# Second mixture's dispatch of half 0 moved into the last three chunks of the state space stage

## The chip, the cores and the metric

The program runs on one core of a Trainium2 chip. The metric is the device time of one execution in microseconds (us), taken as the median of several executions. Five engines run beside each other, each with a queue of its own that is worked off in order: TensorE (PE), VectorE (DVE), ScalarE (ACT), GpSimd (POOL) and SyncE (SP, which here only issues transfers). They wait for each other by semaphores.

## The reference, cut to what matters

4096 rows of 128 numbers pass four layers, each added to its input: an attention, a first mixture of experts, a selective state space layer, and a second mixture of experts. The last two are what the change is about:

```python
x = x + _L1_attn_ref(_layernorm(x, axis=-1), ...)      # state space, 16 states per channel, scan over time
x = x + _L1_ffn_ref(_layernorm(x, axis=-1), ...)       # second mixture
# _L1_ffn_ref, x of shape (4096, 128), 8 experts of width 176, the best 2 taken
scores = jax.nn.softmax(xf @ gate_w.T, axis=-1)
biased = scores + gate_b
_, idx = lax.top_k(biased, K)
w = jnp.take_along_axis(scores, idx, axis=-1) * ROUTER_SCALE
h = jax.nn.silu((xf @ w1 + b1) * (xf @ w3 + b3))       # per chosen expert
y = sum over the 2 chosen experts of w * (h @ w2 + b2)
z = _expert(xf, sw1, sb1, sw3, sb3, sw2, sb2)          # one shared expert for all rows
return y + z
```

The state space layer works on 16 sequences of 256 rows, and no sequence needs another.

## The kernel before

All rows stay in SBUF as `X`: 32 tiles of 128 rows. Half 0 is tiles 0 to 15, half 1 is tiles 16 to 31.

**State space stage** (`state_space`). The 16 sequences are worked on in 8 chunks `c` of two sequences (512 rows, four tiles), so that chunks 0 to 3 are half 0. A chunk has 16 steps `n`, one for each state, in which the two halves `h` of the channels are gone through. In each step ACT makes `dA` by two exponentials (line 1781, three steps ahead), DVE makes `dBu` by two products (1907) and runs two scans into `Hs` (1915, four buffers), POOL multiplies them by `Cb` into `HC` (1871, two buffers), and PE adds `HC` up in PSUM (1621, in `accumulate`, one step later). DVE waits at step `n` for the products `HC` of step `n-4`, POOL waits for PE's sum of step `n-2`. SP loads `Bb` and `Cb` for two steps at a time (`load`), the next `Bb` behind the `Cb` that waits for POOL. Beside that, the queues hold the next chunk's preparation: POOL's four `softplus_step` at steps 3 to 6, PE's projections at steps 0 to 2 and 8 to 10, and at step 2 of a chunk DVE's `gate_rows` of the chunk before (line 1890, `yg`), whose output projection and `update` of `X` (1895) follow at steps 4 and 6. Each `for n in range(N)` loop is written out by Python, so that what stands in it under `if (c, n) == ...` stands at that one place of the engine's queue. After the last step PE, DVE, PE and DVE finish the last chunk one after the other.

**Dispatch of the second mixture** (`dispatch`, a block of its own behind the state space stage). Class `Dispatch` has the steps, each named by its engine. For a half of the rows: DVE takes the mean and variance (`vector_stats`, `vector_variance`), ACT the root, DVE the factor (`vector_scales`) and the normalised rows (`vector_rows`) into `XS`; PE transposes these (`tensor_turn`), ACT copies them (`scalar_copy`), PE multiplies by the router (`tensor_score`); DVE chooses two experts for each row (`vector_keep`, `vector_choose`), PE counts (`tensor_rank`), and DVE works out to which row of the table `rows1` in HBM each row goes (`vector_slots`, `vector_tables`). Then POOL sends the rows: `pool_reweight` puts the first weight beside them, and `pool_scatter` issues one indirect DMA for each of the 16 tiles; then the same for the second choice, when the first 16 have landed. The table was filled with zeros at the kernel's start. The block holds this for half 0 on DVE, ACT, PE and POOL, and for half 1 all but POOL's part.

**Experts** (`experts`). At the start of its block POOL waits until half 0's rows have landed and releases SP (`placed`), which loads 39 tiles of the table; PE, ACT and DVE work them off, while POOL sends half 1's rows by 32 scatters. Half 1's 39 tiles, the shared expert and 64 indirect gathers back into `X` end the program.

A `with nc.Block()` ends for all engines when the last of them is through.

Of the kernel before, what the change touches and what calls it, by code (L numbers as in the profile page):

```python
# [595 lines left out]
class Dispatch:  # L596
# [36 lines left out]
    def over(self, halves, stats, batches, by_scalar, kept_by_scalar):  # L633
# [75 lines left out]

    def tensor_turn(self, pe, k, rows, count):  # L710
# [123 lines left out]
    def pool_reweight(self, pool, h, k):  # L834
# [5 lines left out]
        self.nc.gpsimd.tensor_copy(self.XS[:, half, D], self.rt.c[k][:, half]).then_inc(s.reweighted.sem, 1)  # L840
# [3 lines left out]
    def pool_scatter(self, pool, k, lo, hi, op):  # L844
        for t in range(lo, hi):
            self.nc.gpsimd.indirect_dma_start(self.XG, bass.IndirectOffsetOnAxis(self.rt.slot[k][:, t:t + 1], 0),  # L846
                                              self.XS[:, t, :], None, compute_op=op).then_inc(self.s.sent.sem, 16)


def dispatch(nc, tag, d):  # L850
# [6 lines left out]
    with ExitStack() as ctx:  # L857
        m = Maker(nc, ctx, tag)
        TP = [m.ps(f"TP{v}", [P, d.G * P]) for v in range(2)]
        RP, RK, TT = m.ps("RP", [P, HT * E]), m.ps("RK", [P, HT * E]), m.ps("TT", [P, HT * E])  # L860
        d.place(TP, RP[:], RK[:], TT[:])
        with nc.Block() as block:
            @block.vector
            def _(dve):
                d.vector_stats(dve, 0, HT)
                d.vector_variance(dve, 0, 0, HT)
                d.vector_scales(dve, 0, 0, HT)
                d.vector_rows(dve, 0, HT)
# [14 lines left out]
            def _(act):  # L883
                for h in range(2):
                    d.scalar_root(act, h, h * HT, (h + 1) * HT)
                    for g in range(d.HG):
                        d.scalar_copy(act, h * d.HG + g)
                    d.scalar_power(act, h)

            @block.tensor  # L890
            def _(pe):
                for h in range(2):
                    for g in range(d.HG):
                        k = h * d.HG + g
                        d.tensor_turn(pe, k, d.s.rows, (k + 1) * d.G)
                    if h == 1:
                        pe.wait_ge(d.s.kept.sem, d.s.kept.after(0))
                    for g in range(d.HG):
                        d.tensor_score(pe, h * d.HG + g, g * d.G)
                    if h == 1:  # L900
                        pe.wait_ge(d.s.counted.sem, d.s.counted.after(0))
                    d.tensor_rank(pe, h)
# [1236 lines left out]
```

## Time and profile before

| | us |
|---|---|
| median of 3 runs | 1254.69 |
| lowest, highest | 1253.68, 1259.11 |
| the profiled execution | 1261.0 |
| its span in the trace | 1259.1 |

Busy shares of the span: PE 79%, DVE 75%, POOL 66%, ACT 58%. The span can be cut by stages: the state space stage up to 974 us, the dispatch block from 974 to 1051 us, the experts of the second mixture from 1051 us on. A row of the timeline gives the start, the duration, the engine, the line, what is written from what, and in brackets how long the engine had been idle and what ended that. `x4` is four instructions merged, whose duration is that of all. `SPq` is the queue of transfers that SP issues.

### The profile page before, as it was taken

The numbers are of one execution on the slowest core, as the hardware profiler recorded it, in microseconds if no ns is written. First come the engines' busy times: TensorE is split into PE (matmuls) and PEld (weight loads), VectorE is DVE, ScalarE is ACT, GpSimd is POOL, SyncE is SP. The second block draws the span as 40 slices with busy tenths as digits, with TensorE's granted clock in tenths as the row PEclk, the third lists the DMA queues.
The fourth block names the chain that finished last, engine by engine and source line by source line (L and its number), as shares of the span: only waits on it lengthen the run. The fifth ranks groups of instructions, "written<-read, shape, count | busy, mean of one in ns | idle before, by whom it ended". The sixth has DMA issues, their size and how long they took to land. (4 is left out here: it accounts for less than half of the span.)

```text
span 1259.1 us, 17033 instructions
## 1 busy us (share of the span) xinstructions
PE 998.2 (79%) x4202; PEld 606.3 (48%) x4202; DVE 942.2 (75%) x2310; ACT 735.4 (58%) x1636; POOL 830.8 (66%) x604
## 2 busy tenths in 40 slices
PE   5888867489999978888888888898776335999970
PEld 4666755368888723333333333333222333777750
DVE  6999999653333437999898989999998743777760
ACT  4777747265555568776667676867531113777740
POOL 3333248557247275989898978787975077767676
PEclk9999989599999979999898989989989556999995
DMA  9993012246435343353544443444542014756543
GB/s 271 177 168 124 1 10 24 40 60 92 73 77 94 69 80 104 111 170 116 164 125 153 137 124 126 160 130 140 168 150 67 2 49 76 120 104 123 106 93 64
DMA packets 139137, 133.50 MB, mean 106 GB/s; under 512 B 14579, under 2 KB 120163, under 8 KB 138915
## 3 DMA queue, kind: packets, MB, share of 16 engines
q1 hardware_dynamic: 107106, 115.55, 34.2%
q0 software_dynamic: 31936, 16.86, 11.4%
q8 instruction: 39, 0.64, 0.2%
q14 instruction: 56, 0.45, 0.1%
HBM read 98.66 MB, written 31.60 MB: 103 GB/s over the span
## 5 line engine op out<-in xcount | busy, mean ns | idle before, releaser
L1871 POOL TENSOR_TENSOR ss_HC<-ss_Hs,ss_Cb 128x512 f32<-128x512 f32 x256 | 324.8, 1365 | 85.0 <-PE ss_Y L1621 64.4
L1621 PE MATMUL ss_Y<-ss_HC,g_ident 128*128 128x512 f32 x512 | 270.4, 649 | 47.3 <-POOL ss_HC L1871 41.0
L1915 DVE TENSOR_TENSOR_SCAN ss_Hs<-ss_dA,ss_dBu 128x512 f32<-128x512 f32 x256 | 296.8, 1200 | 7.7 <-ACT ss_dA L1781 7.7
L846 POOL DMA_INDIRECT rows<-m_XS,g_slot x128 | 174.3, 1362 | 61.7 <-issue 34.6
L1781 ACT ACTIVATE ss_dA<-ss_delta,g_A 128x510 f32<-128x510 f32 x256 | 168.3, 712 | 74.1 <-DVE ss_Hs L1915 73.9
L1621 PEld LDWEIGHTS ss_Y<-ss_HC,g_ident 128*128 128x128 f32 x512 | 92.9, 200 | 209.2 <-POOL ss_HC L1871 149.2
L1153 PE MATMUL m_x_UP<-g_m_w,m_x_gT 128*128 (+1 forms) x532 | 193.0, 469 | 0.0
L1907 DVE TENSOR_TENSOR ss_dBu<-ss_duP,ss_Bb 128x512 f32<-128x512 f32 x256 | 163.1, 682 | 10.5 <-DMA ss_Bb<-bc_rows 8.9
L1173 PEld LDWEIGHTS m_x_DP<-g_m_w,m_x_hT 128*128 128x128 f32 x908 | 121.9, 191 | 62.3 <-issue 34.6
L1173 PE MATMUL m_x_DP<-g_m_w,m_x_hT 128*128 (+1 forms) x908 | 140.7, 284 | 2.4 <-ACT m_x_hT L1245 2.3
L1245 ACT ACTIVATE m_x_hT<-m_x_HP 128x256 f32<-128x256 f32 (+1 forms) x188 | 80.3, 427 | 87.7 <-PE m_x_HP L1163 85.9
L1294 DVE SCALAR_TENSOR_TENSOR m_x_hid<-m_x_UP,m_x_G,m_x_sg 128x352 f32<-128x352 f32 x78 | 45.5, 583 | 110.2 <-ACT m_x_sg L1227 110.2
L1133 POOL DMA_INDIRECT g_X<-out_rows,g_slot x64 | 100.4, 1569 | 38.1 <-issue 18.3
L520 POOL TENSOR_TENSOR at_RP<-at_RP,a_rope 128x1024 f32<-128x1024 f32 x16 | 38.4, 2401 | 90.3 <-ACT at_RP L357 90.2
L1153 PEld LDWEIGHTS m_x_UP<-g_m_w,m_x_gT 128*128 128x128 f32 x532 | 87.9, 194 | 18.3 <-issue 1.7
L1163 PE MATMUL m_x_HP<-g_ident,m_x_hid 128*128 128x128 f32 x454 | 80.6, 273 | 2.5 <-DVE m_x_hid L1294 2.5
L1301 DVE TENSOR_TENSOR m_x_sg<-m_x_UP,g_m_b 128x352 f32<-128x352 f32 x110 | 57.7, 524 | 33.2 <-PE m_x_UP L1153 33.1
L1121 POOL DMA_INDIRECT g_X<-out_rows,g_slot x32 | 49.3, 1541 | 44.8 <-DMA out_rows<-m_x_YO 33.6
L1144 PE MATMUL m_x_TP<-g_ident,m_x_G 128*128 128x128 f32 x188 | 52.5, 279 | 30.0 <-DMA m_x_G<-rows 28.8
L1586 PE MATMUL ss_Q<-ss_xpad,ss_w_conv 128*128 128x512 f32 x128 | 60.5, 619 | 5.2 <-ACT ss_xpad L1711 5.2
L1227 ACT ACTIVATE m_x_sg<-m_x_UP 128x352 f32<-128x352 f32 x78 | 36.2, 464 | 39.7 <-PE m_x_UP L1153 39.7
L1163 PEld LDWEIGHTS m_x_HP<-g_ident,m_x_hid 128*128 128x128 f32 x454 | 56.0, 142 | 4.0 <-DVE m_x_hid L1294 2.8
(271 smaller groups left out, 1760.9 us busy)
## 6 DMA issues: line engine op xcount, KB each, us to landing
ss_Bb<-bc_rows SPq DMA_DIRECT2D x64, 512.0 KB, 5.0
ss_Cb<-bc_rows SPq DMA_DIRECT2D x64, 512.0 KB, 4.1
rows<-g_Z SPq DMA_DIRECT2D x2, 5031.0 KB, 48.9
m_x_G<-rows SPq DMA_DIRECT2D x156, 64.5 KB
out_rows<-m_x_YO SPq DMA_DIRECT2D x156, 64.0 KB
g_m_w<-in_w_up SPq DMA_DIRECT2D x1, 2816.0 KB, 11.2
g_m_b<-in_b SPq DMA_DIRECT2D x1, 2160.0 KB, 10.3
g_X<-in_x SPq DMA_DIRECT2D x4, 512.0 KB, 5.8
```

Source lines behind the costliest of these rows:

```text
L846: self.nc.gpsimd.indirect_dma_start(self.XG, bass.IndirectOffsetOnAxis(self.rt.slot[k][:, t:t + 1], 0), self.XS[:, t, :], None, compute_op ...
L1133: nc.gpsimd.indirect_dma_start(X[:, t * D:(t + 1) * D], None, Y[0:(h + 1) * NH * P, :], bass.IndirectOffsetOnAxis(rt.slot[k][:, t:t + 1], ...
L1153: ins = nc.tensor.matmul(UP[v % 2][:, at:at + n], gT[v % 2][:], w.w[:, ds(e + c, n)], start=True, stop=True)
L1163: ins = nc.tensor.transpose(HP[0:n, c * P:(c + 1) * P], hid[v % 2][:, c0:c0 + n], ident[:])
L1173: ins = nc.tensor.matmul(DP[v % 2][:, 0:D], hT[v % 2][0:n, c * P:(c + 1) * P], w.w[0:n, ds(e + WU + c * D, D)], start=c == 0, stop=c == NC ...
L1245: ins = nc.scalar.activation(hT[v % 2][:, 0:full], HP[:, 0:full], ACT.Copy)
L1586: ins = nc.tensor.matmul(dst, w_conv[:, h, k, :], xpad[:, h, :, k:k + S], start=k == 0, stop=k == K)
L1621: ins = nc.tensor.matmul(Yp[:, h, :], ident[:], HC[n % 2][:, h, :], start=False, stop=n == N - 1)
L1781: nc.scalar.activation(dA[n % NA][:, h, :, 1:S], seqs(delta[v][:, h, :])[:, :, 1:S], ACT.Exp, scale=A[:, h, n:n + 1]).then_inc(dA_ready.se ...
L1871: nc.gpsimd.tensor_tensor(HC[n % 2][:, h, :], Hs[n % 4][:, h, :], Cb[g % 2][:, n % 2, :], ALU.mult).then_inc(hc_ready.sem, 1)
L1907: v_.tensor_tensor(dBu[:, h, :], duP[:, h, :], Bb[g % 2][:, n % 2, :], ALU.mult).then_inc(dBu_ready.sem, 1)
L1915: v_.tensor_tensor_scan(Hs[n % 4][:, h, :], dA[n % NA][:, h, :, :].rearrange("p s t -> p (s t)"), dBu[:, h, :], 0.0, ALU.mult, ALU.add).th ...
```

## The change

Half 0's dispatch leaves the block behind the state space stage and is written into the state space loops: at chunk 5 (`OWN - 1`), chunk 6 (`OWN`) and chunk 7 (`LAST`). Eight (`sent`) of its 32 scatters are issued there too, one for each of steps 5 to 12 of chunk 7. In the block that is left, POOL begins at once with the other 24 scatters, and the other engines do half 1's dispatch. The normalised rows of half 0 are now made by ACT (`scalar_rows`), not DVE, with one more DVE instruction (`vector_minus`); groups have four tiles in place of eight; the eight early scatters add to the zeros in the table, the others write. `XS` is split in two tensors. Waiting for the mixture's weights now stands ahead of the state space stage.

```diff
+    def vector_minus(self, dve, lo, hi):
+        self.nc.vector.scalar_tensor_tensor(self.minus[:, lo:hi], self.mv[:, lo:hi, 0], -1.0, self.sc[:, self.n - 1, lo:hi],
+                                            ALU.mult, ALU.mult).then_inc(self.s.scaled.sem, 1)
...
+    def vector_less(self, dve):
+        v, link = self.nc.vector, Chain(dve, self.chain)
+        link(v.tensor_reduce(self.mx[:], self.lg[:], AX.X, ALU.max))
+        v.tensor_tensor(self.ex[:], self.lg[:], self.each(self.mx), ALU.subtract).then_inc(self.s.less.sem, 1)
+
     def vector_choose(self, dve, h):
+        self.vector_less(dve)
+        self.vector_pick(dve, h)
+
+    def vector_pick(self, dve, h):
...
@@ dispatch
             @block.vector
             def _(dve):
-                d.vector_stats(dve, 0, HT)
-                d.vector_variance(dve, 0, 0, HT)
-                d.vector_scales(dve, 0, 0, HT)
-                d.vector_rows(dve, 0, HT)
                 d.vector_stats(dve, HT, T)
                 d.vector_variance(dve, 1, HT, T)
-                d.vector_keep(dve, 0, 0)
-                d.vector_choose(dve, 0)
-                d.vector_slots(dve, 0)
-                d.vector_tables(dve, 0)
                 d.vector_scales(dve, 1, HT, T)
                 d.vector_rows(dve, HT, T)
+                d.vector_tables(dve, 0)
                 d.vector_keep(dve, 1, 1)
                 d.vector_choose(dve, 1)
                 d.vector_slots(dve, 1)
...
             @block.gpsimd
             def _(pool):
-                for k in range(2):
-                    d.pool_reweight(pool, 0, k)
-                    d.pool_scatter(pool, k, 0, HT, ALU.bypass)
+                d.pool_scatter(pool, 0, sent, HT, ALU.bypass)
+                d.pool_reweight(pool, 0, 1)
+                d.pool_scatter(pool, 1, 0, HT, ALU.bypass)
...
@@ state_space, tensor
+                        if (c, n) == (LAST, 0):
+                            d.tensor_rank(pe, 0)
+                        if (c, n) == (LAST, 4):
+                            pe.wait_ge(d.s.counted.sem, d.s.counted.after(0))
...
+                        if (c, n) == (OWN, 7):
+                            pe.wait_ge(x_updated.sem, x_updated.after(c - 1))
+                        if c == OWN and 7 <= n < 7 + d.HG:
+                            d.tensor_score(pe, n - 7, (n - 7) * d.G)
+                        if (c, n) == (OWN, 6):
+                            pe.wait_ge(gate_copied.sem, gate_copied.after(c + 1))
+                        if c == OWN and 6 <= n < 6 + d.HG:
+                            d.tensor_turn(pe, n - 6, d.s.scalar_rows, (n - 5) * d.G)
...
@@ state_space, scalar
+                        if (c, n) == (OWN - 1, 13):
+                            d.scalar_root(act, 0, 0, HT)
+                        if c == OWN and 3 <= n < 3 + d.HG:
+                            d.scalar_rows(act, 0, (n - 3) * d.G, (n - 2) * d.G)
+                        if c == OWN and 7 <= n < 7 + d.HG:
+                            d.scalar_copy(act, n - 7)
+                        if (c, n) == (OWN, 14):
+                            d.scalar_power(act, 0)
...
@@ state_space, gpsimd
+                        if (c, n) == (LAST, 4):
+                            d.pool_reweight(pool, 0, 0)
+                        if c == LAST and 5 <= n < 5 + sent:
+                            d.pool_scatter(pool, 0, n - 5, n - 4, ALU.add)
...
@@ state_space, vector
+                        if (c, n) == (OWN - 1, 12):
+                            d.vector_stats(dve, 0, HT)
+                            d.vector_variance(dve, 0, 0, HT)
+                        if (c, n) == (OWN, 0):
+                            d.vector_scales(dve, 0, 0, HT)
+                            d.vector_minus(dve, 0, HT)
+                        if (c, n) == (OWN, 14):
+                            d.vector_keep(dve, 0, 0)
+                            d.vector_less(dve)
+                        if (c, n) == (LAST, 0):
+                            d.vector_pick(dve, 0)
+                        if (c, n) == (LAST, 3):
+                            d.vector_slots(dve, 0)
```

POOL's queue from chunk 7 of the state space stage to its end. The first fence is of before (L1871 the `HC` products, L846 the scatters of the second mixture, L1133 the last gathers):

```order
L1871 TENSOR_TENSOR ss_HC<-ss_Hs,ss_Cb 128x512 x50
L1527 UNCONDITIONAL_BRANCH
L904 UNCONDITIONAL_BRANCH
L840 COPY m_XS<-g_c 128x16
L846 DMA rows<-m_XS,g_slot 9984x129 x16
L840 COPY m_XS<-g_c 128x16
L846 DMA rows<-m_XS,g_slot 9984x129 x16
L862 UNCONDITIONAL_BRANCH
L1102 UNCONDITIONAL_BRANCH
```

The second is of the change; of the eight pairs of a scatter and its step's products the first two and the last stand here.

```order
L1892 TENSOR_TENSOR ss_HC<-ss_Hs,ss_Cb 128x512 x28
L852 COPY m_XS<-g_c 128x16
L1892 TENSOR_TENSOR ss_HC<-ss_Hs,ss_Cb 128x512 x2
L858 DMA rows<-m_XS,g_slot 9984x129
L1892 TENSOR_TENSOR ss_HC<-ss_Hs,ss_Cb 128x512 x2
L858 DMA rows<-m_XS,g_slot 9984x129
...
L858 DMA rows<-m_XS,g_slot 9984x129
L1892 TENSOR_TENSOR ss_HC<-ss_Hs,ss_Cb 128x512 x6
L1528 UNCONDITIONAL_BRANCH
L902 UNCONDITIONAL_BRANCH
L858 DMA rows<-m_XS,g_slot 9984x129 x8
```

In the second, products of the state space stage stand behind each of the eight scatters, and the block that follows starts with a scatter in place of a wait.

DVE's queue in chunk 7 of the change, from step 3 to step 4: L1932 is `dBu`, L1940 the scans, and between them stands `vector_slots`, of which the first seven and the last two instructions stand here.

```order
L1940 SCALAR_TENSOR_TENSOR ss_Hs<-ss_dA,ss_dBu 128x512 x2
L810 COPY m_d_tot<-ss_Q 128x128
L811 COPY m_d_rk<-ss_Q 128x128
L812 SCALAR_TENSOR_TENSOR m_d_run<-g_masks,m_d_tot 128x128
L814 TENSOR_TENSOR m_d_base<-m_d_run,m_d_tot 128x128
L815 TENSOR_SCALAR m_d_n_i<-m_d_run 128x8
L816 TENSOR_SCALAR m_d_n_i<-m_d_n_i 128x8
L817 CAST m_d_ct<-m_d_n_i 128x8
...
L829 CAST g_slot<-m_d_mx 128x16
L830 CAST g_slot<-m_d_mx 128x16
L1932 TENSOR_TENSOR ss_dBu<-ss_duP,ss_Bb 128x512 x2
L1940 SCALAR_TENSOR_TENSOR ss_Hs<-ss_dA,ss_dBu 128x512 x2
```

Before, the scans of step 3 and the `dBu` of step 4 stood next to each other there.

## Rows read from the trace of the kernel before

**Rows 1.** Stretches: busy us and instructions by engine, PE clock, DMA share, GB/s

```profile
860.00:918.00 58.00, 43.59 (x92) 15.51 (x91) 56.30 (x66) 36.56 (x51) 50.61 (x38) 0.92 0.46 147
1006.00:1051.00 45.00, 10.92 (x50) 10.21 (x50) 16.71 (x66) 3.64 (x4) 30.93 (x33) 0.50 0.14 47
```

**Rows 2.** Timeline of the dispatch block, POOL's rows and SP's first load behind it

```profile
1005.53 1.06 POOL L846 DMA_INDIRECT rows<-m_XS,g_slot  x1 [4.96 <-DVE g_slot L818]
...
1027.39 0.21 POOL L840 COPY m_XS<-g_c 128x16 f32<-128x16 f32 x1 [1.56 <-DMA rows<-m_XS,g_slot]
...
1028.12 0.98 POOL L846 DMA_INDIRECT rows<-m_XS,g_slot  x1 [0.52 <-POOL m_XS L840]
...
1047.20 0.96 POOL L846 DMA_INDIRECT rows<-m_XS,g_slot  x1 [0.30 <-issue]
...
1051.15 4.86 SPq L1076 DMA_DIRECT2D m_x_G<-rows  x6
```

**Rows 3.** Timeline of the dispatch block, DVE's part for half 0

```profile
974.26 3.19 DVE L664 BATCH_NORM_STATS2 m_d_st<-g_X 128x6 f32<-128x128 f32 x16 [0.71 <-PEq L79]
...
979.15 0.25 DVE L685 RECIPROCAL m_d_sc<-m_d_t 128x16 f32<-128x16 f32 x1 [0.28 <-ACT m_d_t L679]
...
980.27 4.19 DVE L700 TENSOR_SCALAR m_XS<-g_X,m_d_mv,m_d_sc 128x128 f32<-128x128 f32 x16
...
993.15 0.29 DVE L756 COPY m_d_lg<-m_f_RP 128x128 f32<-128x128 f32 x1 [4.17 <-PE m_f_RP L735]
...
994.46 0.29 DVE L741 TENSOR_REDUCE m_d_sm<-m_d_ex 128x16 f32<-128x128 f32 x1 [0.37 <-ACT m_d_ex L747]
...
1004.62 0.17 DVE L818 CAST g_slot<-m_d_mx 128x16 int32<-128x16 f32 x1
```

**Rows 4.** Timeline, POOL in two steps of chunk 7, and DVE behind the last step

```profile
945.22 2.49 POOL L1871 TENSOR_TENSOR ss_HC<-ss_Hs,ss_Cb 128x512 f32<-128x512 f32 x2 [0.89 <-DVE ss_Hs L1915]
...
952.06 2.49 POOL L1871 TENSOR_TENSOR ss_HC<-ss_Hs,ss_Cb 128x512 f32<-128x512 f32 x2 [0.89 <-DVE ss_Hs L1915]
...
969.50 1.23 DVE L1890 TENSOR_TENSOR ss_yg<-ss_Y,ss_gate 128x1024 f32<-128x1024 f32 x1 [2.80 <-PE ss_Y L1621]
```

**Rows 5.** Timeline, POOL in chunk 2: a gather between the products of its steps

```profile
655.00 4.95 POOL L1871 TENSOR_TENSOR ss_HC<-ss_Hs,ss_Cb 128x512 f32<-128x512 f32 x4 [0.72 <-PE ss_Y L1621]
660.11 1.57 POOL L1852 DMA_INDIRECT g_X<-out_rows,g_slot  x1 [0.15 <-issue]
661.11 5.50 POOL L1871 TENSOR_TENSOR ss_HC<-ss_Hs,ss_Cb 128x512 f32<-128x512 f32 x4
```

**Rows 6.** Timeline of chunk 0, POOL and DVE: small DVE instructions between the scans

```profile
506.50 2.51 POOL L1871 TENSOR_TENSOR ss_HC<-ss_Hs,ss_Cb 128x512 f32<-128x512 f32 x2
507.15 0.67 DVE L1408 TENSOR_SCALAR sr_ve<-sr_mv 128x8 f32<-128x8 f32 x1
507.74 1.31 DVE L1409 TENSOR_SCALAR sr_ve<-sr_mv 128x8 f32<-128x8 f32 x1
508.95 2.38 POOL L1521 TENSOR_TENSOR ss_delta<-ss_delta,ss_ln 128x1024 f32<-128x1024 f32 x1
508.96 2.40 DVE L1410 COPY g_mean<-sr_mv 128x8 f32<-128x8 f32 x1
```

**Rows 7.** Timeline of chunks 6 and 7: a late load, and PE's and POOL's waits

```profile
896.52 1.30 DVE L1907 TENSOR_TENSOR ss_dBu<-ss_duP,ss_Bb 128x512 f32<-128x512 f32 x2 [1.71 <-DMA ss_Bb<-bc_rows]
...
919.49 3.55 PE L1618 MATMUL ss_Y<-ss_xi,ss_w_D 128*128 128x512 f32 x4 [6.48 <-DVE ss_yg L1890]
...
924.90 12.33 POOL L1871 TENSOR_TENSOR ss_HC<-ss_Hs,ss_Cb 128x512 f32<-128x512 f32 x10 [6.25 <-PE ss_Y L1621]
```

**Rows 8.** Timeline, PE: half 0's transposes and scores in the block, a wait in chunk 6

```profile
982.47 4.02 PE L716 MATMUL m_f_TP<-g_ident,m_XS 128*128 128x128 f32 x16 [9.64 <-DVE m_XS L700]
...
986.28 6.83 PE L735 MATMUL m_f_RP<-g_m_wr,m_d_xT 128*128 128x8 f32 x32
...
885.18 3.64 PE L1621 MATMUL ss_Y<-ss_HC,g_ident 128*128 128x512 f32 x4 [2.40 <-POOL ss_HC L1871]
```

More of the change, by code:

```diff
@@ L649, in over, with row @@
             s.lifts.over(batches)
+    def row(self, t):
+        return self.XS[t // HT][:, t % HT, :]
     def each(self, a):
@@ L706, in scalar_rows @@
         for t in range(lo, hi):
-            self.nc.scalar.activation(self.XS[:, t, 0:D], self.X[:, t * D:(t + 1) * D], ACT.Identity, bias=self.minus[:, t:t + 1],
+            self.nc.scalar.activation(self.row(t)[:, 0:D], self.X[:, t * D:(t + 1) * D], ACT.Identity, bias=self.minus[:, t:t + 1],
                                       scale=self.sc[:, use, t:t + 1]).then_inc(self.s.scalar_rows.sem, 1)
@@ L846, in pool_scatter, with dispatch @@
             self.nc.gpsimd.indirect_dma_start(self.XG, bass.IndirectOffsetOnAxis(self.rt.slot[k][:, t:t + 1], 0),
-                                              self.XS[:, t, :], None, compute_op=op).then_inc(self.s.sent.sem, 16)
-def dispatch(nc, tag, d):
+                                              self.row(t), None, compute_op=op).then_inc(self.s.sent.sem, 16)
+def dispatch(nc, tag, d, sent):
     with ExitStack() as ctx:
         m = Maker(nc, ctx, tag)
-        TP = [m.ps(f"TP{v}", [P, d.G * P]) for v in range(2)]
+        TP = [m.ps(f"TP{v}", [P, d.G * P]) for v in range(d.HG)]
         RP, RK, TT = m.ps("RP", [P, HT * E]), m.ps("RK", [P, HT * E]), m.ps("TT", [P, HT * E])
@@ L883, in _ @@
             def _(act):
[L884 to L888, printed above, removed]
+                d.scalar_root(act, 1, HT, T)
+                for k in range(d.HG, 2 * d.HG):
+                    d.scalar_copy(act, k)
+                d.scalar_power(act, 1)
             @block.tensor
             def _(pe):
[L892 to L902, printed above, removed]
+                for g in range(d.HG):
+                    d.tensor_turn(pe, d.HG + g, d.s.rows, (g + 1) * d.G)
+                for g in range(d.HG):
+                    d.tensor_score(pe, d.HG + g, g * d.G)
+                d.tensor_rank(pe, 1)
             @block.gpsimd
             def _(pool):
-                for k in range(2):
-                    d.pool_reweight(pool, 0, k)
-                    d.pool_scatter(pool, k, 0, HT, ALU.bypass)
+                d.pool_scatter(pool, 0, sent, HT, ALU.bypass)
+                d.pool_reweight(pool, 0, 1)
+                d.pool_scatter(pool, 1, 0, HT, ALU.bypass)
 class TileSignals:
@@ L924, in over, with experts @@
         self.y_ready.over(routed)
-def experts(nc, tag, signals, d, inside, X, XS, rt, XG, Y, out, n_early, w, gated, ident, ahead=None):
+def experts(nc, tag, signals, d, inside, X, rt, XG, Y, out, n_early, w, gated, ident, ahead=None):
     n_shared, scale_col, H = w.n_shared, w.ns, w.H
@@ L1070, in fetch @@
                     if t.shared:
[L1071 removed]
+                        sp.dma_start(G[v][:, 0:D], d.row(t.i)[:, 0:D]).then_inc(arrived[v], 16)
                     else:
@@ L1464, in state_space @@
         Q = [m.ps(f"Q{v}", [P, CH]) for v in range(2)]
+        d.place([Q[1]], Q[0][:, 0:HT * E], Q[0][:, HT * E:2 * HT * E], Q[0][:, 2 * HT * E:3 * HT * E])
+        OWN, LAST = NCH - 2, NCH - 1
         padded, cleared, weights_ready = m.sem("padded"), m.sem("cleared"), m.sem("weights_ready")
```

35 lines of the change are left out of this document (16 added, 19 removed).

## The prediction

> **What bounds the kernel now.** I cut the span into stretches first. In chunk 6 DVE is busy for 56.30 of 58.00 us, so it sets the pace of the state space stage and anything given to DVE there is paid in full; POOL has 50.61 of the 58. In the later part of the dispatch block only POOL works much, DVE for 16.71 of 45 us [rows 1]. Then the timelines of that block. DVE begins half 0 at 974.26 [rows 3]; POOL issues its first scatter at 1005.53, comes to the second set of 16 at 1028.12 and ends its last at 1048.16; SP's first load for the experts follows at 1051.15 [rows 2]. So the block costs 76.9 us: 31.3 in which POOL waits for slots, 42.6 of POOL, 3.0 of block end. Nothing of the experts can start earlier, since POOL's queue stands in front of the block's end. The stage behind it is not touched by the change: the same 39 tiles, the same 32 scatters, the same gathers. It shifts as a whole.
>
> **The block: what is taken out.** A scatter's pitch is (1047.20 - 1028.12) / 15 = 1.27 us. Before, 16 scatters and their landing took 1027.39 - 1005.53 = 21.86 us [rows 2]. Now POOL starts with the block, with 8: 21.86 - 8 x 1.27 = 11.7. The weights' copy and the wait behind it take 0.73 (1027.39 to 1028.12), the other 16 take 20.04 (to 1048.16), the end of the block 2.99. Sum 35.5, from 76.9: **41.4 us less**. Beside it DVE does for half 1 what it did for half 0, from 974.26 to 1004.79 [rows 3], 30.5 us and a little over 1 for the tables at its end; half 0's tables lie in its wait for the scores (4.17 us idle at 993.15). That is 32, and POOL's own part is 11.7 + 0.7 + 20.0 = 32.5. POOL stays last, but by less than 1 us: more scatters moved out would bring nothing.
>
> **The state space stage: DVE's own time.** By [rows 3]: statistics and variance, 974.26 until DVE went idle at 978.87, 4.6; the factor 979.15 to 980.27, 1.1, and one more small instruction for `minus`, 0.2; from keeping the scores (993.15) to the slots (1004.79) 11.64, less a wait for ACT of 0.37, 11.3. Together **17.2 us**. ACT takes over the 16 row instructions (4.19 on DVE). No slack covers the 17.2.
>
> **Waits for POOL inside DVE's inserted instructions.** [Rows 6] show small DVE instructions between scans while POOL multiplies. They take 0.67, 1.31 and 2.40 us, where one of their kind takes 0.2 otherwise, and each ends with the POOL instruction beside it: at 507.82, 509.05 and 511.36, while POOL's end at 507.75, 509.01 and 511.33. So such an instruction waits for the POOL instruction in progress, and POOL takes its next before DVE's next comes. `dBu` and the scans themselves, which read PSUM, don't suffer. What can be lost at one place is bounded by what POOL has left to do, since without new scans it runs dry. In step with DVE, POOL starts its pair of products at the first scan's end and needs 2.49 us [rows 4], so it is busy about 1.3 us beyond the second scan. I take 0.6 for the statistics (only the last instruction is of the kind), 1.1 for the factor, 0.8 each for keeping the scores and for the choice. The slots are dearer: PE's sum waits for `gate_rows` at step 2 (919.49), and POOL's pair of step 2 starts only at 924.90 [rows 7]; DVE has then finished the scans of step 3 (919.4 + 2.3 + 3.42 = 925.1). POOL has four products left, 5.0 us. Two copies from PSUM take 0.5; the next four instructions, 1.1 us by themselves, wait for one product each, 4.5: 3.4 more. Sum **6.7 us**; from below it is 0, from above 12 (two pairs left at each place where I set one).
>
> These prices rest on copies and scalar operations, the only kinds in [rows 6], while most inserted instructions combine two tensors in SBUF. I take them as alike. The Trainium skill, "SBUF — State Buffer", Who interferes with whom, holds that a VectorE instruction with two SBUF inputs and a GpSimd one that reads SBUF exclude each other too. By it the term stands; if only copies and scalar operations were blocked it would be an estimated 4 us (0.6, 0.5 for the factor, 2.8 for three instructions of the slots).
>
> **The eight scatters.** POOL's time for one between products comes from a gather of the same form, which adds too: [rows 5] have four products in 4.95 us up to 659.95, one gather, and four products up to 666.61, so 6.66 - 4.95 = 1.71 us. The bound below is the writing scatter's 1.27 [rows 2], that above the gather's 1.57 with the gap of 0.30 that scatters showed, 1.87. A step of DVE is (952.06 - 945.22) / 2 = 3.42 [rows 4]; POOL's is 2.48 + 1.71 = 4.19 in steps 5 to 12. It falls behind by 8 x 0.77 = 6.2 us, under the three steps that DVE may run ahead, so DVE doesn't stall; in the last two steps it regains 2 x 0.94. What is left, **4.3 us**, delays the last product, and PE, `yg` and the output wait for it one after the other [rows 4]. Bounds 0.6 and 5.4.
>
> **What costs nothing.** ACT: two table loads, 16 row instructions, four copies and a power in steps where it is busy for 36.56 of 58 us [rows 1], three steps ahead of DVE. PE: 4.02 us of transposes and 6.83 of scores [rows 8], at the half clock of the block (0.50, [rows 1], that is 1.2 GHz); chunk 6 ran at 0.92 of 2.4 GHz. They stand at steps 6 to 10 of chunk 6, about 2.7 us in a step, where PE had idled 2.40 for POOL [rows 8]. Cover is POOL's pace; if it goes, the third rival. `tensor_rank` stands in front of PE's last sum of chunk 6, but DVE, whose marks it awaits, reaches the gate that wants the sum only two steps later. The barrier for the weights only changes its place.
>
> **Sum.** -41.4 + 17.2 + 6.7 + 4.3 = -13.2 us. The profiled execution took 1261.0, so it would be 1247.8, with a span of 1245.9. That execution was 6.3 us above the median of the runs, 1254.69; the difference laid on the median gives **1241.5**.
>
> **Rivals.**
> *No waiting for POOL.* The inserted instructions run as in the block: -41.4 + 17.2 + 4.3 = -19.9, 1234.8. For it: POOL is in step with DVE at chunk 7 and runs dry during the choice. Against it: [rows 6]. Chance 0.14.
> *PE's work delays POOL in chunk 6.* POOL works off its backlog there without a pause, SP's `Cb` waits for POOL, and the next `Bb` stands behind it; DVE already waited 1.71 us for one [rows 7], so there is no spare. If all 10.85 us of PE less the 2.40 idle pass through, DVE loses 8.5 more: 1250.0. Against it: the late `Bb` hangs on a product of step 7, and on sums from before the first scores. Chance 0.13.
> *DVE holds up the scatters in the block.* The 24 scatters now lie wholly beside half 1's DVE work. If POOL could not issue during the 16 row instructions of 4.19 us [rows 3], the block is 4.2 longer: 1245.7. Against it: before, the first 16 scatters ran beside just these instructions of half 1 and took (21.86 - 1.56) / 16 = 1.27 each, no more than the second 16, which DVE's work accompanied only at first [rows 2]. The Trainium skill, "SBUF — State Buffer", SBUF: two separate sides, warns of this: transfers issued from GpSimd starve while VectorE copies in its fast mode. By that rule the rival holds; the rows speak against it. Chance 0.05.
> *Slower: an adding scatter holds POOL in chunk 7.* No scatter that adds to HBM stands between products before. If each held POOL for 1.71 + 2.4 us, POOL's step would be 6.6 us, DVE would run out of its three steps, and 8 x 2.4 = 19.2 us come on top: 1260.7, slower. Below 3.4 us for one the change still gains. Against it: the adding gather of [rows 5] and its 0.15 us gap. Chance 0.04.
>
> **How the numbers follow.** The forecast has 0.60, and by itself lies between 1237 and 1247 (contention 3 to 11, tail 3 to 5); 0.04 is for what I don't see. A measurement can tell about 0.5% from no change, so below 1248.4 is faster and above 1261.0 slower. Faster: 0.60 + 0.14 + 0.05 and nearly half of the third case's 0.13, 0.84. Same: the rest of that case and of the unseen, 0.11. Slower 0.05. The range for 8 in 10 takes in most of the first rival, 1233, and reaches to the end of the PE case, 1250.
>
> **What the profile after would show.** The block from DVE's first statistics to SP's first load: 35.5 us. POOL's scatters there at 1.27, in chunk 7 about 1.7 between products. DVE's `vector_slots` in chunk 7 some 7 to 8 us in place of 4.4, with single instructions of over 1 us that end with a product. POOL's idle time gone from steps 5 to 15 of chunk 7, and DVE waiting some 7 us for PE in front of the last `yg` where it waited 2.80 [rows 4]. I'd be wrong if DVE waited for `Bb` in chunk 6 longer than 1.71, if the choice's instructions all waited, or if the experts' stage changed its length.

## The result, and the profile after

| | before | changed |
|---|---|---|
| median, us | 1254.69 (1252.41 to 1263.62, 11 runs) | 1248.93 (1244.82 to 1256.56, 11 runs) |
| ratio of times | | 0.9936, 95% interval 0.9913 to 0.9959 |
| profiled execution, us | 1261.0 | 1248.62 |
| its span, us | 1259.1 | 1246.8 |

The change is faster, by the ratio 8.0 us (5.1 to 10.9) of 1254.69; gains below are worked out from ratios in the same way, and the medians alone can differ from them by a few us (5.8 here). The forecast was 13.2 less and 1241.5; its range of 1233 to 1250 holds the time, but the gain is about six tenths of what was forecast, and the median lies just above the 1248.4 below which the forecast called a time faster. The two profiled executions, on the other hand, differ by 12.4. Most of this study is about that gap.

The stretches of the changed kernel, cut at the gates (columns as in [rows 1]). The gate of a chunk is its `yg` instruction, which stands at step 2 of the next chunk. The first three stretches are the three chunks in which half 0's dispatch now lies, the third with what finishes the state space stage, and the fourth is the block that is left:

```profile
802.80:867.50 64.70, 53.11 (x124) 20.75 (x124) 63.03 (x106) 48.04 (x72) 49.05 (x37) 0.95 0.38 131
867.50:935.80 68.30, 50.06 (x138) 23.24 (x138) 64.11 (x90) 41.80 (x67) 48.22 (x37) 0.80 0.35 124
935.80:1004.20 68.40, 48.70 (x100) 17.55 (x100) 58.56 (x77) 13.64 (x22) 48.88 (x38) 0.82 0.34 92
1004.20:1040.00 35.80, 8.13 (x50) 6.84 (x50) 22.39 (x103) 5.46 (x8) 23.74 (x25) 0.60 0.13 45
```

From gate to gate the chunks took 59.7, 58.2 and 51.3 us before, and 64.7, 68.3 and 64.0 now (the third stretch above runs 4.4 us beyond its gate, to the block). DVE is busy in 63.03 of 64.70, the same share as before, and in 64.11 of 68.30, so that it now idles for 4.2 us in chunk 6 where it idled for 1.7. PE's granted clock fell, from 0.92 in [rows 1] to 0.80 in chunk 6.

The block, in the timeline of the changed kernel: POOL's first two scatters, the weights' copy, the first and the last scatter of half 1, SP's load, and the scores of half 1 with DVE's wait for them. They answer to [rows 2].

```profile
1004.22 3.19 DVE L665 BATCH_NORM_STATS2 m_d_st<-g_X 128x6 f32<-128x128 f32 x16 [0.32 <-PEq L1528]
1004.84 1.01 POOL L858 DMA_INDIRECT rows<-m_XS,g_slot  x1 [6.29 <-SPq L874]
1006.16 0.98 POOL L858 DMA_INDIRECT rows<-m_XS,g_slot  x1 [0.30 <-issue]
...
1015.16 3.97 PE L740 MATMUL m_f_RP<-g_m_wr,m_d_xT 128*128 128x8 f32 x32
1016.24 0.21 POOL L852 COPY m_XS<-g_c 128x16 f32<-128x16 f32 x1 [1.44 <-DMA rows<-m_XS,g_slot]
1016.98 0.98 POOL L858 DMA_INDIRECT rows<-m_XS,g_slot  x1 [0.52 <-POOL m_XS L852]
...
1019.17 0.29 DVE L761 COPY m_d_lg<-m_f_RP 128x128 f32<-128x128 f32 x1 [3.58 <-PE m_f_RP L740]
...
1036.30 0.96 POOL L858 DMA_INDIRECT rows<-m_XS,g_slot  x1 [0.30 <-issue]
...
1040.04 4.75 SPq L1074 DMA_DIRECT2D m_x_G<-rows  x6
```

It is 35.8 us from DVE's first statistics to SP's load, where 35.5 was forecast, and the scatters' pitch is (1036.30 - 1016.98) / 15 = 1.29. PE's scores and DVE's wait of 3.58 us for them lie beside POOL's work and cost nothing.

The slots in chunk 7, timeline of DVE. The four instructions from 943.99 on are the ones that pay:

```profile
943.79 0.16 DVE L815 TENSOR_SCALAR m_d_n_i<-m_d_run 128x8 int32<-128x8 f32 x1
943.99 1.28 DVE L816 TENSOR_SCALAR m_d_n_i<-m_d_n_i 128x8 int32<-128x8 int32 x1
945.30 1.19 DVE L817 CAST m_d_ct<-m_d_n_i 128x8 f32<-128x8 int32 x1
946.52 1.31 DVE L819 TENSOR_TENSOR m_d_base<-m_d_base,m_d_rk 128x128 f32<-128x128 f32 x1
947.76 1.24 DVE L820 TENSOR_TENSOR_SCAN m_d_end<-g_masks,m_d_ct 128x8 f32<-128x8 f32 x1
949.03 0.17 DVE L821 TENSOR_TENSOR m_d_first<-m_d_end,m_d_ct 128x8 f32<-128x8 f32 x1
...
951.13 1.29 DVE L1932 TENSOR_TENSOR ss_dBu<-ss_duP,ss_Bb 128x512 f32<-128x512 f32 x2
```

POOL in the same chunk, and DVE at its end (it answers to [rows 4]):

```profile
943.98 4.98 POOL L1892 TENSOR_TENSOR ss_HC<-ss_Hs,ss_Cb 128x512 f32<-128x512 f32 x4 [7.04 <-PE ss_Y L1622]
953.71 2.49 POOL L1892 TENSOR_TENSOR ss_HC<-ss_Hs,ss_Cb 128x512 f32<-128x512 f32 x2 [4.75 <-DVE ss_Hs L1940]
...
959.77 1.60 POOL L858 DMA_INDIRECT rows<-m_XS,g_slot  x1 [0.15 <-issue]
960.85 3.06 POOL L1892 TENSOR_TENSOR ss_HC<-ss_Hs,ss_Cb 128x512 f32<-128x512 f32 x2
964.07 1.60 POOL L858 DMA_INDIRECT rows<-m_XS,g_slot  x1 [0.16 <-issue]
...
990.65 7.91 POOL L1892 TENSOR_TENSOR ss_HC<-ss_Hs,ss_Cb 128x512 f32<-128x512 f32 x6
...
999.84 1.22 DVE L1915 TENSOR_TENSOR ss_yg<-ss_Y,ss_gate 128x1024 f32<-128x1024 f32 x1 [7.01 <-PE ss_Y L1622]
```

POOL's four products of 4.98 us start at 943.98, and beside each of them one DVE instruction takes about 1.2 us, a cast of 128x8 that takes 0.17 elsewhere (1028.16, in the block) as much as the rest. When the products end, at 948.96, so does the waiting. Then the scatters: 1.60 us each, a step of POOL 4.3 us, and DVE waits 7.01 us at the end where it waited 2.80.

### The profile page after: what moved, and what is told of

It is laid out like the page before. It is cut to its first block and busy times, and to the rows that moved or that the text cites. A ratio compares the mean times of both kernels' runs of the same rounds, so it can differ in the third digit from the quotient of the medians.

```text
span 1246.8 us, 17047 instructions
## 1 busy us (share of the span) xinstructions
PE 997.9 (80%) x4202; PEld 601.3 (48%) x4202; DVE 944.8 (76%) x2295; ACT 742.0 (60%) x1656; POOL 836.3 (67%) x604
## 5 line engine op out<-in xcount | busy, mean ns | idle before, releaser
L1892 POOL TENSOR_TENSOR ss_HC<-ss_Hs,ss_Cb 128x512 f32<-128x512 f32 x256 | 330.5, 1416 | 97.2 <-PE ss_Y L1622 76.1
L1622 PE MATMUL ss_Y<-ss_HC,g_ident 128*128 128x512 f32 x512 | 281.0, 670 | 53.3 <-POOL ss_HC L1892 47.7
L1940 DVE TENSOR_TENSOR_SCAN ss_Hs<-ss_dA,ss_dBu 128x512 f32<-128x512 f32 x256 | 297.0, 1201 | 7.5 <-ACT ss_dA L1794 7.4
L858 POOL DMA_INDIRECT rows<-m_XS,g_slot x128 | 179.3, 1401 | 61.9 <-issue 34.1
L1622 PEld LDWEIGHTS ss_Y<-ss_HC,g_ident 128*128 128x128 f32 x512 | 95.4, 206 | 218.0 <-POOL ss_HC L1892 158.5
L1932 DVE TENSOR_TENSOR ss_dBu<-ss_duP,ss_Bb 128x512 f32<-128x512 f32 x256 | 163.1, 682 | 12.0 <-DMA ss_Bb<-bc_rows 10.3
## 6 DMA issues: line engine op xcount, KB each, us to landing
g_m_b<-in_b SPq DMA_DIRECT2D x1, 2160.0 KB, 10.5
```

Of the source, the lines that this page charges most:

```text
L1622: ins = nc.tensor.matmul(Yp[:, h, :], ident[:], HC[n % 2][:, h, :], start=False, stop=n == N - 1)
L1892: nc.gpsimd.tensor_tensor(HC[n % 2][:, h, :], Hs[n % 4][:, h, :], Cb[g % 2][:, n % 2, :], ALU.mult).then_inc(hc_ready.sem, 1)
L1932: v_.tensor_tensor(dBu[:, h, :], duP[:, h, :], Bb[g % 2][:, n % 2, :], ALU.mult).then_inc(dBu_ready.sem, 1)
L1940: v_.tensor_tensor_scan(Hs[n % 4][:, h, :], dA[n % NA][:, h, :, :].rearrange("p s t -> p (s t)"), dBu[:, h, :], 0.0, ALU.mult, ALU.add).th ...
```

## The experiments

The stretch by which I compare profiles is **the region**: from the gate of chunk 4 (its `yg`, at 802.82 in the changed kernel) to SP's first load of the experts. In the profiled executions it was 250.9 us before and 237.2 changed, 13.6 less before rounding. Ahead of the region the change only moves the wait for the mixture's weights, yet the gate came anywhere from 798.6 to 805.5 us in the twelve profiles of this study. From the first DVE instruction of the state space stage to this gate all twelve take 358.0 to 358.6 us, so the shift arises in the stages ahead of it, which no run here changes. Behind the region the time was 206.3 to 208.6. So one profiled time against another says little below 7 us, and the region is read instead.

**The kernel before and the changed one again, as they are.**

> The kernel before, unchanged, once more with a profile. It shows how long the stretch that the change touches (from the gate of chunk 4 at step 2 of chunk 5 to SP's first load for the experts) is in another execution: 250.9 us in the first profile. Theory A, that the first profiled execution happened to have late loads that others lack: the stretch is 3 to 6 us shorter here, and the rest of the span the same. Theory B, that the stretch is always 250.9 and the change simply gains less in executions without the profiler: the stretch repeats within 1 us. Ratio to the kernel before within 0.3% of 1 by both.

> The changed kernel, unchanged, once more. By my sum 13 us less than before, ratio 0.9895; by the first measurement 0.9936. The stretch from chunk 5 to SP's first load was 237.2 us in its first profile. Theory A expects it to vary by some us with the waits for Bb in chunks 5 and 6 (5.0 us in the first profile), theory B that it repeats within 1 us.

Before: 1258.13 us, ratio 1.0000 (0.9978 to 1.0022). Changed: 1250.54, ratio 0.9921 (0.9894 to 0.9948), so 9.9 us faster (6.6 to 13.3). The changed kernel's region was 237.5, as the first time. The one of before was not: 246.3, 4.6 shorter than in the first profile. 3.3 of it lie behind the last gate (78.4 in place of 81.7) and 1.2 in chunk 5 (58.5 for 59.7). Theory A had the size right and the cause for the smaller part only: of the late loads, DVE's wait for `Bb` in chunk 5 was 1.37 in place of 2.34, but the 3.3 hang on no load. Theory B, that the stretch repeats, falls. Two more profiles of the same kernel show whether this returns.

> The kernel before, unchanged, a third profile. By theory the stretch from the last gate to SP's first load is either 81.6 us (score matmuls at the half clock, 6.8 us) or 78.4 (full clock, 3.7 us), nothing else.

> The kernel before once more, for its profile. Either the 32 scores take 6.8 us and DVE waits 4.2 for them, the block from the last gate to SP's load is 81.7 us; or they take 3.7, the wait is 1.1 and the block 78.4. Nothing between is expected; if a third length comes, the account by the scores is not complete.

The third profile gave 81.8 behind the last gate (region 251.1), and the fourth 78.3 (region 246.3). I call the first kind the long form and the second the short form. Timeline of the fourth profile: PE's scores of half 0, DVE's wait for them, POOL's first scatter and SP's load.

```profile
984.08 3.72 PE L735 MATMUL m_f_RP<-g_m_wr,m_d_xT 128*128 128x8 f32 x32
...
987.84 0.29 DVE L756 COPY m_d_lg<-m_f_RP 128x128 f32<-128x128 f32 x1 [1.06 <-PE m_f_RP L735]
...
1000.24 1.06 POOL L846 DMA_INDIRECT rows<-m_XS,g_slot  x1 [4.97 <-DVE g_slot L818]
...
1045.64 8.49 SPq L1076 DMA_DIRECT2D m_x_G<-rows  x8
```

Against [rows 3] and [rows 8] the same 32 matmuls took 3.72 us for 6.83, and DVE waited 1.06 for 4.17; everything behind has its old distance (first scatter 12.40 us behind the copy of the scores, 12.38 before). The stretches around the scores show the clock, first in the profile of before, then in the fourth profile (columns as in [rows 1]):

```profile
982.00:993.00 11.00, 10.45 (x48) 10.05 (x48) 6.91 (x43) 3.33 (x3) 0.00 (x0) 0.50 0.01 1
```

```profile
980.00:988.00 8.00, 7.45 (x48) 6.96 (x48) 6.87 (x43) 3.33 (x3) 0.00 (x0) 0.71 0.01 2
```

At 0.50 PE was granted 1.2 GHz throughout; at 0.71 it got 2.4 GHz for a part, the scores among it.

**The kernel before, with PE kept at work ahead of the transposes.**

```diff
@@ dispatch, tensor
+                for _ in range(40):
+                    nc.tensor.transpose(TP[1][:, 0:P], d.ident[:], d.ident[:])
                 for h in range(2):
```

> The kernel before with 40 added transposes of the identity at the head of PE's queue in the dispatch block, where PE waits for half 0's rows (output unchanged). In the first profile of before the 32 score matmuls of half 0 took 6.83 us at the half clock and DVE waited 4.17 us for them; in the second they took 3.73 us and DVE waited 1.08. Theory, that before loses 3.1 us in executions where PE's clock falls in that wait: here they take 3.7 us in every execution, DVE waits 1.1, and the kernel is 0 to 3 us faster than before (0.1% on average). Rival, that the clock there does not hang on what PE does in the wait: 6.83 us may come again.

Scores 3.72 us, DVE's wait 1.06, 78.5 behind the last gate, region 246.4: the short form again. But in time it was 1258.88 against 1260.09, ratio 0.9991 (0.9970 to 1.0012), 1.1 us faster and not told from none. Were the long form the usual one, about 3 us should have shown; the interval, 3.8 faster to 1.5 slower, leans against it and doesn't exclude it.

**The kernel before, with half 0's scores issued twice** (64 matmuls; the added ones write the same values).

```diff
-        for t in range(self.G):
+        for t in list(range(self.G)) * times:
...
-                        d.tensor_score(pe, h * d.HG + g, g * d.G)
+                        d.tensor_score(pe, h * d.HG + g, g * d.G, 2 - h)
```

> The kernel before with half 0's 32 score matmuls of the dispatch block issued twice (64). If they lie on the path to POOL's first scatter, as I hold since the block's length followed them (81.7 us from the last gate to SP's load when the 32 took 6.83 us, 78.4 when they took 3.73), the block grows by one more set: 3.2 to 3.7 us when they run at the full clock, 6.4 to 6.9 when at half, DVE's wait for them from 1.1 or 4.2 us to 4.7 or 11, and the time by 3 to 7 us (ratio 1.0025 to 1.0055). The rival, by which the block's length has another cause and the scores only change beside it: block 78.4 or 81.7 as before, ratio 1.000.

1265.33 us against 1256.28, ratio 1.0067 (1.0043 to 1.0091): 8.4 us slower (5.4 to 11.4). Timeline of PE and DVE:

```profile
987.70 10.57 PE L735 MATMUL m_f_RP<-g_m_wr,m_d_xT 128*128 128x8 f32 x64
...
998.31 0.29 DVE L756 COPY m_d_lg<-m_f_RP 128x128 f32<-128x128 f32 x1 [7.89 <-PE m_f_RP L735]
```

And PE's clock in it, by stretches (columns as in [rows 1]):

```profile
987.70:991.00 3.30, 3.30 (x33) 3.30 (x31) 2.65 (x24) 2.31 (x2) 0.00 (x0) 1.00 0.00 0
991.00:994.50 3.50, 3.50 (x20) 3.50 (x19) 0.00 (x0) 0.00 (x0) 0.00 (x0) 0.51 0.00 0
```

About the first half of the 64 ran at 2.4 GHz and the second at 1.2: 10.57 is one set of 3.7 and one of 6.9. Behind the last gate it took 85.2 us, 6.9 more than the short form. That the scores lie on the path to the scatters in the kernel before is thereby shown, and their price with them. I had expected that both sets would run at one level, with 3 to 7 us. In this one profile the second half ran at the lower level; whether the other executions had 10.57 us too, or both halves at the lower level, isn't known, so the run doesn't tell which form of the block is the usual one.

**The change with no scatters in chunk 7.**

```diff
-        sent = HT // 2
+        sent = 0
```

> The change with sent = 0: half 0's dispatch stays in the state space stage, but all 32 scatters are issued in the block. My theory: the tail of chunk 7 goes (4.2 us less in front of the last gate, where DVE waits 2.8 instead of 7.0), and the block is 8 x 1.27 = 10.2 us longer, 46.0 in place of 35.8; together 6.0 us slower than the change, about 0.5% above it. Rival, that the adding scatters cost as much in chunk 7 as they spare in the block: same time as the change.

1253.70 against 1258.78, ratio 0.9974 (0.9952 to 0.9996), which is 6.7 us slower than the changed kernel's 0.9921 beside it. Timeline, DVE at the last gate and POOL's first scatter:

```profile
993.63 1.23 DVE L1915 TENSOR_TENSOR ss_yg<-ss_Y,ss_gate 128x1024 f32<-128x1024 f32 x1 [2.81 <-PE ss_Y L1622]
...
998.67 1.06 POOL L858 DMA_INDIRECT rows<-m_XS,g_slot  x1 [6.33 <-SPq L874]
```

The wait at the last gate is back at 2.81: the 7.01 comes from the eight scatters. Behind the gate 50.5 us stand for 40.2, 10.3 more, eight times 1.28. So the eight take 4.2 and give 10.3, which is 6.1 us of gain. The region, 244.5, is 7.3 longer than the change's. Not all of that is the scatters': chunks 5 and 6, ahead of the first of them, are together 1.9 longer (65.9 and 69.0 for 64.7 and 68.3), and chunk 7 is 4.8 shorter.

**The slots at step 1 of chunk 7, where POOL has less in hand.**

```diff
-                        if (c, n) == (LAST, 3):
+                        if (c, n) == (LAST, 1):
                             d.vector_slots(dve, 0)
```

> The change with vector_slots at step 1 of chunk 7 in place of step 3. My theory: its 8.5 us are 4.4 of its own and 4.1 of waiting for the four products that POOL has left at step 3; at step 1 POOL has one pair left at most, so it takes 5.5 to 6.7 us and single instructions over 1 us are one or two in place of four; the kernel is 2 to 3 us faster than the change (0.2%). Rival, that these instructions are slow inside the state space stage wherever they stand (semaphores, queue): still 8 us, no gain.

1250.88, ratio 0.9939 (0.9912 to 0.9965), the same as the changed kernel. The slots did get cheaper, 5.6 us (931.12 to 936.69) in place of 8.5, with two of POOL's products beside them and not four. The rest of the expectation fell, as the timeline of POOL and DVE shows:

```profile
930.90 2.60 POOL L1892 TENSOR_TENSOR ss_HC<-ss_Hs,ss_Cb 128x512 f32<-128x512 f32 x2 [8.41 <-PE ss_Y L1622]
944.95 7.43 POOL L1892 TENSOR_TENSOR ss_HC<-ss_Hs,ss_Cb 128x512 f32<-128x512 f32 x6 [11.45 <-PE ss_Y L1622]
...
995.35 1.23 DVE L1915 TENSOR_TENSOR ss_yg<-ss_Y,ss_gate 128x1024 f32<-128x1024 f32 x1 [8.99 <-PE ss_Y L1622]
```

The slots at step 3 had held DVE while POOL worked off its backlog, so that POOL was in step when the scatters began. At step 1 DVE is held while POOL is idle too, 11.45 us; POOL then enters the scatters some 2 us late and hands them on: 8.99 at the gate for 7.01. The region is 236.3, 0.9 less than the change's, where 2 to 3 had been expected.

**The same, and four scatters in POOL's idle time of step 1, four at steps 7 to 10.**

```diff
-                        if (c, n) == (LAST, 4):
+                        if (c, n) == (LAST, 1):
                             d.pool_reweight(pool, 0, 0)
-                        if c == LAST and 5 <= n < 5 + sent:
-                            d.pool_scatter(pool, 0, n - 5, n - 4, ALU.add)
+                            d.pool_scatter(pool, 0, 0, 4, ALU.add)
+                        if c == LAST and 7 <= n < 11:
+                            d.pool_scatter(pool, 0, n - 3, n - 2, ALU.add)
```

> The change with vector_slots and the weights' copy at step 1 of chunk 7, four of the eight scatters right behind, where POOL waits 7 us for PE before its pair of step 2, and the other four at steps 7 to 10. My theory (tail = POOL's lag at the last step, 0.77 us for each scatter less 0.94 for each step without one): the tail goes, DVE waits 2.8 to 3.5 us before the last gate in place of 7.0 to 7.4; with 3 us for the slots the stretch from chunk 5 to SP's first load is 230 to 231 us in place of 237.3; ratio to before 0.986 to 0.988. Rival, that scatters cost DVE wherever they stand: 235 or more.

1245.06 (1239.4 to 1246.0) against 1260.09, ratio 0.9889 (0.9860 to 0.9917), 14.0 us faster than before (10.5 to 17.6): the lowest ratio of all kernels here. Its interval overlaps the change's, so that it beats the change rests on the region as much as on the time. Region 230.9, 6.4 less than the change's, and in the range expected. Timeline of POOL, and of DVE at the gate:

```profile
944.72 1.60 POOL L858 DMA_INDIRECT rows<-m_XS,g_slot  x1 [3.77 <-DVE g_slot L830]
946.62 1.57 POOL L858 DMA_INDIRECT rows<-m_XS,g_slot  x1 [0.30 <-issue]
...
952.76 12.31 POOL L1892 TENSOR_TENSOR ss_HC<-ss_Hs,ss_Cb 128x512 f32<-128x512 f32 x10 [0.86 <-issue]
...
981.75 10.36 POOL L1892 TENSOR_TENSOR ss_HC<-ss_Hs,ss_Cb 128x512 f32<-128x512 f32 x8
992.63 2.48 POOL L1892 TENSOR_TENSOR ss_HC<-ss_Hs,ss_Cb 128x512 f32<-128x512 f32 x2 [0.52 <-DVE ss_Hs L1941]
...
996.40 1.23 DVE L1916 TENSOR_TENSOR ss_yg<-ss_Y,ss_gate 128x1024 f32<-128x1024 f32 x1 [2.80 <-PE ss_Y L1622]
```

The first four scatters fill time in which POOL waits, with the slots at step 1, for the gate's sum (11.45 us above), and behind the last of the other four there are five steps in which POOL catches up. The pair at 992.63 waits for DVE again, and the gate's wait is 2.80, as before the change.

**The change with PE's transposes and scores of half 0 issued twice, in chunk 6.**

```diff
-                            d.tensor_score(pe, n - 7, (n - 7) * d.G)
+                            d.tensor_score(pe, n - 7, (n - 7) * d.G, 2)
...
-                            d.tensor_turn(pe, n - 6, d.s.scalar_rows, (n - 5) * d.G)
+                            d.tensor_turn(pe, n - 6, d.s.scalar_rows, (n - 5) * d.G, 2)
```

> The change with each transpose and each score matmul of half 0 in chunk 6 issued twice (same output), 4 to 5 us more for PE in steps 6 to 10. The change has a wait of 2.7 us for Bb at step 12 of chunk 6 in both profiles, where before had 1.4 to 1.7. Theory, that it comes from POOL's pair of step 2 starting 8.2 us behind the gate in place of 5.6 (PE at the half clock there), not from the scores: it stays at 2.7, and the time is that of the change. Rival (the third of the prediction), that the scores delay POOL: the waits in chunk 6 grow by 3 us or more.

1246.25, ratio 0.9908 (0.9877 to 0.9940): not slower than the change. The region is 237.0, as the change's 237.2 and 237.5. Chunk 6 took 66.8 us, where it took 68.3 and 67.8 in the two profiles of the changed kernel. Timeline, one of PE's four doubled sets of scores, and DVE's waits for `Bb`:

```profile
889.07 1.85 PE L740 MATMUL ss_Q<-g_m_wr,m_d_xT 128*128 128x8 f32 x16
...
895.04 1.30 DVE L1932 TENSOR_TENSOR ss_dBu<-ss_duP,ss_Bb 128x512 f32<-128x512 f32 x2 [1.44 <-DMA ss_Bb<-bc_rows]
...
902.99 1.30 DVE L1932 TENSOR_TENSOR ss_dBu<-ss_duP,ss_Bb 128x512 f32<-128x512 f32 x2 [1.00 <-DMA ss_Bb<-bc_rows]
```

That is 2.4 us of waiting for `Bb` in the chunk, where the changed kernel's profiles have 3.6 and 2.7. Twice the work on PE did not delay POOL, so the rival of PE's work falls.

## Why the prediction was right, and why its sum was too large

**The block.** Right: 35.8 us for 35.5, POOL last, all 24 scatters at the pitch forecast, beside DVE's row instructions. The rival of DVE holding up the scatters falls. The Trainium skill, "SBUF — State Buffer", SBUF: two separate sides, warned here of transfers that starve beside VectorE's fast mode. No starving shows: the pitch was 1.29 us. In which mode the row instructions ran the trace doesn't tell, so it neither bears the rule out nor refutes it.

**DVE's own time and the waits for POOL.** Right. The five places, from first instruction to the next `dBu`, took in the changed kernel's profile, own time by the same instructions in the block:

| | taken | own | lost | forecast lost |
|---|---|---|---|---|
| statistics, 842.50 | 4.5 | 4.5 | 0 | 0.6 |
| factor, 860.67 | 2.2 | 1.3 | 0.9 | 1.1 |
| keeping the scores, 916.26 | 1.3 | 0.9 | 0.4 | 0.8 |
| choice, 924.40 | 6.8 | 6.0 | 0.8 | 0.8 |
| slots, 942.62 | 8.5 | 4.4 | 4.1 | 3.4 |
| sum | 23.3 | 17.1 | 6.2 | 6.7 |

The pattern is that of [rows 6]: in the slots one small instruction is lost to each product that POOL still had to do. Instructions with both inputs in SBUF lose as copies do: L819 and L820 at 946.52 and 947.76, 1.31 us for 0.29 and 1.24 for 0.17. The Trainium skill, "SBUF — State Buffer", Who interferes with whom, says so of two SBUF inputs, and the trace agrees. The statistics lost nothing: the aggregate took 1.17 beside POOL's products as in the block. The rival without these waits falls. The nearness of the two sums hides misses of up to 0.7 us in single places.

**The eight scatters.** Right: a wait of 7.01 for 2.80, 4.2 us for 4.3. The run without them confirms both sides, what they take and what they give. An adding scatter took 1.56 to 1.60 us between products, as the gather did; the slower rival falls. Two small misses cancel in the 4.2: the eight scatters and the eleven pairs of products from step 5 on took 41.4 us (957.12 to 998.55), where the forecast's prices give 41.0, and DVE's `update` of `X` at step 6, 0.6 us between two of its steps, was left out of DVE's pace.

**What costs nothing.** Nearly. PE's added work cost nothing, but the first of the forecast's signs of being wrong came: DVE waited for `Bb` in chunk 6 longer than 1.71 us. (The other two did not: one of the choice's instructions waited, and the experts' stage kept its length, 206.8 us for 208.0.) What DVE's added work does to PE was missed: PE stands idle while DVE works alone, and its clock falls. The sum of chunk 6 that the gate's products wait for, in the changed kernel's timeline, POOL's pair behind it, and DVE's later wait for `Bb`:

```profile
868.76 3.78 PE L1619 MATMUL ss_Y<-ss_xi,ss_w_D 128*128 128x512 f32 x4 [4.60 <-DVE ss_yg L1915]
...
875.67 2.50 POOL L1892 TENSOR_TENSOR ss_HC<-ss_Hs,ss_Cb 128x512 f32<-128x512 f32 x2 [7.75 <-PE ss_Y L1622]
...
905.98 1.30 DVE L1932 TENSOR_TENSOR ss_dBu<-ss_duP,ss_Bb 128x512 f32<-128x512 f32 x2 [2.75 <-DMA ss_Bb<-bc_rows]
```

And in the profile of before:

```profile
861.73 1.98 PE L1618 MATMUL ss_Y<-ss_xi,ss_w_D 128*128 128x512 f32 x4
...
865.57 2.50 POOL L1871 TENSOR_TENSOR ss_HC<-ss_Hs,ss_Cb 128x512 f32<-128x512 f32 x2 [3.10 <-PE ss_Y L1621]
```

3.78 us for 1.98 is the lower level for the upper. It is so in every profile here: in the six kernels with the change PE has been idle for 4.6 us ahead of this sum, and the sum takes 3.78; in the six others it has not been idle, and the sum takes 1.98. The pair of step 2 comes 8.2 us behind the gate in place of 5.6 (7.0 in the second profile of the changed kernel). With it 2.75 + 0.82 us of waiting for `Bb` in chunk 6 took the place of 1.71, 1.9 more; 1.0 more in the second profile. That the late pair causes that wait is argued from SP's queue, where a `Bb` stands behind a `Cb` that waits for POOL. No run took the clock alone away, and in the run with PE's work doubled this same sum also took 3.78. So the cause of the later `Bb` is not shown. In the sum over the three chunks this miss is hidden by luck: they grew by 27.8 us where 28.2 was forecast, since in chunk 5 DVE waited 1.43 for `Bb` in place of 2.34, and its 0.70 ahead of the gate was gone.

**The step that failed: the 76.9 us that the block costs before.** The forecast set its terms against the profiled execution and laid the difference of -13.2 on the median of 1254.69, which was 6.3 below that execution. I named those 6.3 and took them for nothing that touches the block. In fact, between profiles of the kernel before, 4.6 us lie inside the region: in the block PE's 32 scores stand on the path to POOL's first scatter, at 6.83 us in two profiles and at 3.7 in two others (and in the warmed kernel), and chunk 5 is 1.2 shorter in the second kind. The change takes those scores off the path: in its block the scores of half 1 took 3.97 in one profile and 6.84 in the other, and behind the last gate it has 40.2 and 40.1 us. So it saves, by the regions of these profiles,

- from the long form 13.6 us (250.9 to 237.2), the forecast's 13.2,
- from the short form 246.3 - 237.2 = 9.1 us.

The two timed ratios give 8.0 (5.1 to 10.9) and 9.9 us (6.6 to 13.3). Both intervals hold 9.1, and both exclude 13.6. The other kernels with the change agree: the six ratios (8.0 and 9.9; 3.3 with no scatters in chunk 7, 7.7 with the slots at step 1, 14.0 with the scatters spread, 11.6 with PE's work doubled) average 9.1 us, and their six regions lie on average 9.1 below the short form's 246.3 and 13.6 below the long one's 250.9. The warmed kernel, which by theory always has the short form (one profile shows it) and was only 1.1 us faster than the kernel before (3.8 faster to 1.5 slower), points the same way: the short form seems the more frequent. That is concluded from times; no run counted the forms. With 73.6 in place of 76.9 for the block (the fourth profile, 972.07 to 1045.64) the forecast's own terms come to -9.9, and with chunk 5's 1.2 as well to -8.7, which would be 1246.0; measured 1248.9. What stays open: what decides in which form an execution runs, how often each comes (four profiles of the unchanged kernel, two of each), and the rest of the absolute time, 2.9 us, which is less than the chance shifts ahead of the region. The absolute times can't decide it: the profiled executions took 1261.0 and 1262.6 us in the long form and 1253.8 and 1253.9 in the short one, and the medians of the kernel before lay between, at 1254.7 to 1260.1. Chunk 5 has two lengths in the changed kernel too (64.7 and 65.8), so its 1.2 comes and goes with or without the change.

## What to carry to other kernels

Before a profiled difference is laid on a median, look for steps of the path that depend on a state that differs from run to run; here one group of small matmuls behind idle time had two prices. Small instructions given to DVE here paid up to one product's time for every product that POOL still had in hand, so a long group belongs where the neighbour has run dry, but what the neighbour does next must be counted too: the cheap place for the slots gave back what it saved until four scatters were put in the same gap. A queue that must catch up needs steps left behind the last thing added: five behind four scatters left no tail here, where three behind eight left 4.2 us.

## What the runs showed of the hardware that I had not expected

- What a DVE instruction lost beside a POOL product was the same for a small and a larger one: a cast of 128x8 (0.17 us alone) took 1.19 and one of 128x128 with two inputs (0.29) took 1.31. `BATCH_NORM_AGGREGATE` (1.17 for sixteen beside POOL's products and 1.17 in the block) was not slowed, nor `TENSOR_REDUCE` (0.29 at 916.55 beside a product and 0.29 at 1019.49 in the block), nor were copies from PSUM (0.26 and 0.29 beside products, with the slots at step 1).
- A scatter that adds has a pitch of 1.88 us back to back (944.72, 946.62, 948.50, 950.35 in the spread version), one that writes 1.27; between products both the adding scatter (1.60) and the gather (1.57) leave POOL's step at 4.2 to 4.3.
- 32 score matmuls at the same place of the same kernel took 6.83 us or 3.72, and 64 took 10.57, about half at 2.4 and then half at 1.2 GHz. Twice the work on PE in chunk 6 left the chunk 1.0 to 1.5 us shorter, with a granted clock of 0.88 for 0.80 and 0.81, and the region as long as it was.
